# Sparse attention: the 64th largest score of a row found by counting on ScalarE, five units under way, in place of sixteen chunk searches and eight rounds on VectorE

## The chip, the cores and the metric

The kernel runs on one core of a Trainium2 chip. The metric is the device time of one execution in microseconds (us), the median of several runs. PE is TensorE, DVE is VectorE, ACT is ScalarE, POOL is GpSimd, SP is SyncE; PEld is a weight load on PE.

## The reference, cut to what matters

The program is a chain of nine attention, mixture and token layers over `h`, 4 batch rows of 1536 tokens of 64 numbers. The change touches one layer, the sparse attention of layer 2. Its input is `_layernorm(h)`:

```python
value = jnp.einsum('bnd,ed->bne', x, W) + b
norm = jnp.linalg.norm(x, axis=-1, keepdims=True)
normed_x = x / jnp.maximum(norm, EPS)
cos_sim = jnp.einsum('bnd,bmd->bnm', normed_x, normed_x)
topk_vals, topk_inds = jax.lax.top_k(cos_sim, TOP_K)          # TOP_K = 64
attn_sparse = jnp.zeros_like(cos_sim).at[b_idx, n_idx, topk_inds].set(topk_vals)
attn = jax.nn.softmax(attn_sparse, axis=-1)
return jnp.einsum('bnm,bmd->bnd', attn, value)
```

So every token has a row of 1536 similarities; the 64 largest keep their value, the others become 0 (and still count as exp(0) in the softmax).

## The kernel before, in words

A loop takes the four batch rows one after the other (a pass each) through phases; at the end of a phase every engine drains and waits for the others on the semaphore `phase_left`. The order of work inside a phase is written out by hand, engine by engine, and engines meet on counted semaphores (`ph.mark`, `ph.after`). Two phases matter here. `sim2` makes the normed rows `y`, their transpose `qt` (64 partitions by 1536) and `kt`, a copy of it. `attn2` is the sparse attention: 12 units of 128 query tokens.

For unit `u` of `attn2` (functions `attn_pe`, `attn_act`, `attn_vec` with `kind == "attn2"`):

- PE makes three banks of scores (L616) two units ahead; ACT copies the 1536 scores to SBUF (`copy_row`, L760) into one of two row buffers.
- DVE finds the threshold (`maxima`). The row is cut in 16 chunks of 96; each chunk gives its 16 largest by MAX8, MATCH_REPLACE8, MAX8 (L792, L794, L796, `candidates`), 256 candidates together. Eight rounds of MAX8 and MATCH_REPLACE8 over the candidates (L833, L837) give the 64 largest. The chunk searches of unit `u + 1` are issued between the rounds of unit `u`. L842 to L849 test whether the answer could be wrong (`unsure`).
- L850 writes `sparse` = score where it is at least the 64th largest, else 0. PE sums `unsure` over the partitions (L697), DVE loads the sum in a register (L853) and branches: if any row is unsure, the whole 128x1536 tile is searched anew by eight rounds over all 1536 columns (L858, L860). Then `sparse_ready` (L865).
- ACT takes exp of `sparse` with a row sum (L748); PE transposes the result in three groups of four (L645), ACT copies each group (L728), and PE multiplies with the values (L655, the probabilities stationary). DVE scales and adds to `h` (L1102).

## Time and profile before

| | |
|---|---|
| median of 3 runs | 5515.0 us (5504.31 to 5516.92) |
| the profiled execution | 5489.0 us, its span 5487.2 us |
| mean granted TensorE clock | 0.835 |
| busy share of the span | PE 77%, DVE 61%, ACT 35%, POOL 9% |
| one pass of `attn2` in the profile | 701.0 to 984.9 us; four passes |
| DMA | 26.68 MB, mean 5 GB/s |

The profiled execution is 26 us shorter than the median of the three runs. An engine that is busy for a large share of the span bounds the kernel only in the stages in which the others wait for it.

### The profile page before, as it was taken

How to read it: one execution, taken by the hardware profiler on the slowest of the kernel's cores; microseconds unless marked ns; L12 is line 12 of the kernel's file. 1: busy time of each engine (PE TensorE's matmuls, PEld its weight loads, DVE VectorE, ACT ScalarE, POOL GpSimd, SP SyncE). 2: the span in 40 equal slices, each digit the busy share in tenths (PEclk: the TensorE clock that was granted, in tenths of full speed). 3: DMA queues.
4: the chain of work that ended last, by engine and by line, in shares of the span. 5: the costliest groups of instructions: out<-in, count | busy, mean ns of one | idle time of the engine just before them, and what ended most of it. 6: DMA issues, size and time to landing. Idle time of an engine off the chain costs nothing.

```text
span 5487.2 us, 72618 instructions
## 1 busy us (share of the span) xinstructions
PE 4234.8 (77%) x26536; PEld 2887.6 (53%) x26536; DVE 3325.4 (61%) x9095; ACT 1899.6 (35%) x3407; POOL 479.0 (9%) x816
## 2 busy tenths in 40 slices
PE   6885855899887845799888855799888855699987
PEld 4663634565555634555555634555646534555646
DVE  4555689355545679455554779555555769555555
ACT  3341612254341612144332622144432522134432
POOL 0101000101100000011100000011100000021100
PEclk9898955799898965699988966699988976699998
DMA  2000000000000000000000000000000000000000
GB/s 82 5 0 16 4 13 1 1 1 1 1 1 4 1 16 1 1 1 1 1 1 4 1 16 1 1 1 1 1 1 4 1 1 1 1 1 1 1 1 4
DMA packets 28333, 26.68 MB, mean 5 GB/s; under 512 B 10550, under 2 KB 26934, under 8 KB 27450
## 3 DMA queue, kind: packets, MB, share of 16 engines
q1 hardware_dynamic: 27962, 21.98, 1.4%
q8 instruction: 203, 3.33, 0.3%
q14 instruction: 168, 1.38, 0.1%
HBM read 20.40 MB, written 1.57 MB: 4 GB/s over the span
## 4 chain that ended last, share of the span: by engine, by line
PE 52%; DVE 31%; POOL 4%; issue 3%; ACT 2%; DVEq 1%; SPq 0%; POOLq 0%; ACTq 0%
PE ps L605 11%; PE ps L645 7%; DVE qup L794 4%; PE ps L672 4%; PE ps L1622 3%; PE ps L1638 3%; DVE x L792 3%; DVE x L796 3%; DVE ctxt L837 3%; DVE ctxt L833 3%; POOL st L396 2%; PE ps L950 2%; PE ps L608 2%; DVE row_max L1082 2%; PE ps L979 2%
## 5 line engine op out<-in xcount | busy, mean ns | idle before, releaser
L645 PE MATMUL ps<-cst,big 128*128 128x128 f32 x4608 | 660.7, 294 | 313.1 <-ACT big L748 250.3
L645 PEld LDWEIGHTS ps<-cst,big 128*128 128x128 f32 x4608 | 567.7, 153 | 354.8 <-ACT big L748 254.3
L728 ACT COPY big<-ps 128x512 f32<-128x512 f32 x816 | 477.9, 586 | 700.0 <-PE ps L645 696.9
L752 ACT ACTIVATE big<-ps,negmax 128x1024 f32<-128x1024 f32 (+1 forms) x672 | 599.5, 898 | 263.0 <-DVE negmax L867 262.9
L867 DVE TENSOR_REDUCE negmax<-ps 128x1 f32<-128x1536 f32 x336 | 589.9, 1758 | 38.0 <-PE ps L612 18.4
L411 PE MATMUL ps<-cst 128*128 128x512 f32 x608 | 326.9, 697 | 128.0 <-DVEq L187 58.2
L605 PE MATMUL ps<-kup,qup 128*128 128x512 f32 (+3 forms) x768 | 356.3, 561 | 42.1 <-POOLq L187 41.0
L396 POOL TENSOR_TENSOR st<-st,cst 128x6 f32<-128x6 f32 x104 | 156.7, 1507 | 2642.1 <-DVE st L384 2638.0
L424 ACT COPY xt<-ps 64x512 f32<-64x512 f32 x144 | 78.1, 580 | 807.5 <-PE ps L416 807.4
L672 PE MATMUL ps<-big,v 128*32 128x128 f32 (+1 forms) x8064 | 321.9, 277 | 8.1 <-DVE ctxt L1106 6.0
L605 PE MATMUL ps<-klo,qlo 128*128 128x512 f32 (+3 forms) x672 | 313.7, 550 | 3.8 <-DVE big L728 1.5
L411 PEld LDWEIGHTS ps<-cst 128*128 128x128 f32 x608 | 133.4, 227 | 289.6 <-issue 228.7
L760 ACT COPY big<-ps 128x1536 f32<-128x1536 f32 x48 | 69.0, 1438 | 623.3 <-DVE ctxt L865 605.1
L672 PEld LDWEIGHTS ps<-big,v 128*32 128x32 f32 (+1 forms) x8064 | 233.5, 113 | 63.1 <-ACT big L728 53.5
L1082 DVE TENSOR_REDUCE row_max<-ps 128x1 f32<-128x512 f32 (+3 forms) x384 | 213.0, 588 | 76.6 <-PE ps L950 48.9
L655 PEld LDWEIGHTS ps<-v,big 128*128 128x128 f32 x1152 | 254.7, 330 | 0.0
L655 PE MATMUL ps<-v,big 128*128 128x64 f32 x1152 | 252.5, 408 | 0.0
L1986 DVE TENSOR_TENSOR big<-big,ps 85x512 f32<-85x512 f32 x192 | 130.5, 683 | 197.3 <-ACT big L1389 156.8
L728 DVE COPY big<-ps 128x512 f32<-128x512 f32 x336 | 229.0, 682 | 27.1 <-PE ps L645 27.1
L1622 PE MATMUL ps<-cst,big 85*128 85x64 f32 x1536 | 196.1, 285 | 48.7 <-DVE res L1977 48.7
L806 DVE COPY_PREDICATED ps<-cst,ps 128x128 f32<-128x128 int32 x192 | 57.0, 297 | 290.1 <-PE ps L630 290.1
L1622 PEld LDWEIGHTS ps<-cst,big 85*128 85x128 f32 x1536 | 199.4, 204 | 63.1 <-issue 52.9
(321 smaller groups left out, 7413.3 us busy)
## 6 DMA issues: line engine op xcount, KB each, us to landing
rw<-in_w_route SPq DMA_DIRECT2D x128, 64.5 KB, 1.9
cst<-in_consts SPq DMA_DIRECT2D x1, 2671.0 KB, 14.8
cst<-in_consts SPq DMA_DIRECT2D x1, 2670.5 KB, 8.9
big<-in_consts SPq DMA_DIRECT2D x1, 1872.5 KB, 22.1
out_dram<-res SPq DMA_DIRECT2D x4, 384.0 KB, 2.8
experts_in<-in_consts SPq DMA_DIRECT2D x1, 1360.0 KB, 17.6
qup<-in_patches SPq DMA_DIRECT2D x4, 260.0 KB
klo<-in_pe_low SPq DMA_DIRECT2D x2, 384.0 KB, 23.5
```

Of the source, the lines that this page charges most:

```text
L396: nc.gpsimd.tensor_tensor(st[:, 4, t], st[:, 3, t], K("half")[:, t], ALU.pow).then_inc(*ph.mark("rstd_ready"))
L411: nc.tensor.matmul(ps[:, bank, :], ident, K("pos"), start=True, stop=True)
L605: ins = nc.tensor.matmul(bank[:, (a - lo) * P:(b - lo) * P], qq[:, s, qs], kk[:, s, a * P:b * P], start=True, stop=True)
L645: ins = nc.tensor.transpose(turned_bank(kind, u, g)[:, i * P:(i + 1) * P], prob[:, slot_of(kind, u), (4 * g + i) * P:(4 * g + i + 1) * P], ...
L655: ins = nc.tensor.matmul(ps[:, 7, 448:448 + D], pt[:, slot_of(kind, u), g, (i % 4) * P:(i % 4 + 1) * P], v[:, i, :], start=(i == 0), stop= ...
L672: ins = nc.tensor.matmul(ps[w * s:w * s + w, 6, 0:P], v[:, i, at:at + w], pt[:, u % 2, i // 4, (i % 4) * P:(i % 4 + 1) * P], start=(i < n) ...
L728: copy(pt[:, slot_of(kind, u), g, 0:n], turned_bank(kind, u, g)[:, 0:n]).then_inc(*ph.mark(copier(kind, g)))
L752: nc.scalar.activation(prob[:, slot_of(kind, u), cols], src[:, cols], ACT.Exp, bias=bias, accum_out=part_sum[:, u, k:k + 1]).then_inc(*ph. ...
L794: ins = nc.vector.match_replace(work_c, best[:, 0:8], row_c, -4.0)
L867: nc.vector.tensor_reduce(negmax[:, u:u + 1], flat[:, 0:n], AX.X, ALU.max, negate=True)\
L1082: nc.vector.tensor_reduce(row_max[:, lo // 4, unit:unit + 1], ps[:, 5 + n % 2, 0:(hi - lo) * P], AX.X, ALU.max)\
L1622: ins = nc.tensor.matmul(ps[:, 4 + t, e * D:(e + 1) * D], hh[:, n % 2, c, t * P:(t + 1) * P], K("w2_4")[:, (2 * e + c) * D:(2 * e + c + 1) ...
```

## The change

`attn2` gets functions of its own (`sparse_pe`, `sparse_act`, `sparse_vec`), and the 64th largest value is found in another way. For a threshold, ACT computes sign(threshold - score) over the row of 1536 with a running sum (L872 of the new file): the sum tells how many scores lie above it. The first threshold comes from the mean and the deviation of the row (from moments of `y`, not from the scores); DVE then moves it by interpolation between the two ends of a bracket (`move`, some 14 operations on 128 x n numbers, n up to 4), four times at most, until 57 to 64 scores lie above it. After the fifth count one MAX8 over the scores below the threshold gives the values from there to the 64th largest (`select`). If a row of the tile ends outside 57 to 64, the whole tile goes the old way by the eight rounds over 1536 columns. Five units are under way at once: in slot `s` ACT makes the first count of unit `s`, the second of `s - 1`, to the fifth of `s - 4`; then the exp of unit `s - 5`, whose `select` stood in slot `s - 1`, and the copy of row `s + 1`. Six row buffers hold the scores. PE transposes all 12 blocks in one go, ACT copies two of the three banks in one instruction and DVE the third, and the product with the values has the values stationary, as in the other attentions. There are 17 slots for 12 units.

```diff
+PASSES = 5
+ROWS_HELD = PASSES + 1
+START_Z, BRACKET_Z = 1.712, 0.4
+START_COUNT = 40.0
+KEEP = 0.7
...
-        row_copy = (big[:, S:2 * S], big[:, 3 * S:4 * S])
-        sparse = qup[:, 1, :]
+        sparse = work
         qt = qlo[:, 0, :]
-        kt = qlo[:, 1, :]
+        row_copy = (held[:, 0, :], held[:, 1, :], big[:, S:2 * S], big[:, 3 * S:4 * S], qlo[:, 1, :], qup[:, 1, :])
...
+        def counts_in(s):
+
+            return [(s - k + 1, k) for k in (4, 3, 2, 1, 5) if 0 <= s - k + 1 < T]
...
+        def moving(s):
+
+            return max(0, s - PASSES + 2), min(s + 1, T)
...
+        def sparse_pe(ph, pe):
...
+            for t in range(T):
+                ins = nc.tensor.matmul(ps[:, 6 + t // 6, (t % 6) * (D + 1):(t % 6 + 1) * (D + 1)], qt[0:D, t * P:(t + 1) * P],
+                                       moments[0:D, :], start=True, stop=True)
...
+            for s in slots():
+                u, last = s - PASSES, s - PASSES + 1
+                if u >= 0:
+                    pe.wait_ge(*ph.after("probs_ready", u + 1))
...
+                    for i in range(T):
+                        ins = nc.tensor.transpose(ps[:, 3 + i // 4, (i % 4) * P:(i % 4 + 1) * P], prob[:, 0, i * P:(i + 1) * P], ident)
+                    ins.then_inc(*ph.mark("pt_psum"))
+                if s + 2 < T:
+                    scores(s + 2)
+                if u >= 0:
...
+                    for i in range(T):
+                        ins = nc.tensor.matmul(ps[D * (i % 2):D * (i % 2) + D, 6, 0:P], v[:, i, :],
+                                               pt[:, 0, i // 4, (i % 4) * P:(i % 4 + 1) * P],
+                                               start=(i < 2), stop=(i >= T - 2), skip_group_check=True)
+                    ins.then_inc(*ph.mark("strips_ready"))
+                if 0 <= last < T:
+                    pe.wait_ge(*ph.after("unsure_ready", last + 1))
+                    nc.tensor.matmul(ps[:, 7, 0:1], K("mean"), unsure, start=True, stop=True).then_inc(*ph.mark("unsure_summed"))
...
+        def sparse_act(ph, act):
...
+            for s in slots():
+                u = s - PASSES
+                for i, (unit, k) in enumerate(counts_in(s)):
+                    if i == 0:
+                        act.wait_ge(*ph.after("thresholds_ready", s + 1))
+                        act.wait_ge(*ph.after("row_copied", min(s, T - 1) + 1))
...
+                    nc.scalar.activation(counted_out[n % 3], row_copy[unit % ROWS_HELD], ACT.Sign, scale=-1.0, bias=cur[:, 0, unit:unit + 1],
+                                         accum_out=signs[:, unit:unit + 1]).then_inc(*ph.mark("counted"))
+                if u >= 0:
+                    act.wait_ge(*ph.after("sparse_ready", u + 1))
...
+                    nc.scalar.activation(prob[:, 0, :], sparse, ACT.Exp, accum_out=rowsum[:, u:u + 1]).then_inc(*ph.mark("probs_ready"))
+                if s + 1 < T:
+                    copy_row(s + 1)
+                if u >= 0:
+                    act.wait_ge(*ph.after("pt_psum", u + 1))
...
+                    nc.scalar.copy(pt[:, 0, 0:2, :].rearrange("p g n -> p (g n)"), ps[:, 3:5, :].rearrange("p b n -> p (b n)"))\
...
+            def move(s):
...
+                dve.wait_ge(*ph.after("counted", counted_by(s) - (1 if s >= PASSES - 1 else 0)))
...
+            def select(u, s):
...
+                link(nc.vector.scalar_tensor_tensor(work, row, cur[:, 0, u:u + 1], row, ALU.is_lt, ALU.mult))
+                link(nc.vector.max(below[:, 1:9], work))
...
+                link(nc.vector.scalar_tensor_tensor(sparse, row, pick[:, 0:1], row, ALU.is_ge, ALU.mult))
...
-                Phase(led, "attn2").leave(pool)
+                ph = Phase(led, "attn2")
+                pool.wait_ge(*ph.after("var_ready", 1))
+                nc.gpsimd.tensor_tensor(st[:, 4, :], st[:, 3, :], K("half")[:, T:2 * T], ALU.pow).then_inc(*ph.mark("deviation"))
+                ph.leave(pool)
...
                         link(nc.gpsimd.memset(qup[0:D, :, S - 1:S], 0.0))
+                        link(nc.gpsimd.memset(qlo[D:P, 1, :], 0.0))
...
+                for t in range(T):
+                    ins = nc.tensor.matmul(ps[0:D, 0, 0:D], y[:, t, :], y[:, t, :], start=(t == 0), stop=(t == T - 1))
+                ins.then_inc(*ph.mark("square_psum"))
...
-                for j in range(NB):
-                    dve.wait_ge(*ph.after("xt_copied", NB + j + 1))
-                    nc.vector.tensor_copy(kt[0:D, 512 * j:512 * (j + 1)], qt[0:D, 512 * j:512 * (j + 1)])
+                dve.wait_ge(*ph.after("xt_copied", 2 * NB))
+                link(nc.vector.tensor_reduce(moments[0:D, D:D + 1], qt[0:D, :], AX.X, ALU.add))
+                nc.vector.tensor_scalar(moments[0:D, D:D + 1], moments[0:D, D:D + 1], 1.0 / S, None, ALU.mult)
+                dve.wait_ge(*ph.after("square_psum", 1))
+                link(nc.vector.tensor_scalar(moments[0:D, 0:D], ps[0:D, 0, 0:D], 1.0 / S, None, ALU.mult))
```

In the order of the instructions, ACT in the middle of `attn2` before, two units (copy of a row, exp, three group copies):

```order
L760 COPY big<-ps 128x1536 [waits sparse_ready,scores_ready]
L748 ACTIVATE big,rowsum<-qup 128x1536 [waits pt_psum,sparse_ready]
L728 COPY big<-ps 128x512 [waits ctx_ready,pt_psum] x3
L760 COPY big<-ps 128x1536 [waits sparse_ready,scores_ready]
L748 ACTIVATE big,rowsum<-qup 128x1536 [waits pt_psum,sparse_ready]
```

and in the change, one full slot (L872 is a count, L878 the exp, L860 the copy of a row, L885 the copy of two banks):

```order
L872 ACTIVATE y,ctxt<-qlo,ctxt 128x1536 [waits counted,row_copied,thresholds_ready]
L872 ACTIVATE sq,ctxt<-qup,ctxt 128x1536 [waits counted]
L872 ACTIVATE x,ctxt<-held,ctxt 128x1536 [waits counted]
L872 ACTIVATE y,ctxt<-held,ctxt 128x1536 [waits counted]
L872 ACTIVATE sq,ctxt<-big,ctxt 128x1536 [waits counted]
L878 ACTIVATE big,rowsum<-qup 128x1536 [waits pt_psum,sparse_ready]
L860 COPY big<-ps 128x1536 [waits sparse_ready,scores_ready]
L885 COPY big<-ps 128x1024 [waits strips_ready,pt_psum]
```

Five counts have come ahead of the exp; the first waits for the thresholds that DVE moved, and no table load stands between them.

PE for one unit before (L616 scores, L697 the sum of `unsure`, L645 transposes, L655 the product with the values):

```order
L616 MATMUL ps<-qlo 128x512 [waits row_copied]
L616 MATMUL ps<-qlo 128x512 x2
L697 MATMUL ps<-ctxt,cst 128x1 [waits unsure_ready]
L645 MATMUL ps<-cst,big 128x128 [waits pt_by_act,probs_ready]
L645 MATMUL ps<-cst,big 128x128 x3
L645 MATMUL ps<-cst,big 128x128 [waits pt_by_act]
L645 MATMUL ps<-cst,big 128x128 x3
L655 MATMUL ps<-big,v 128x64 [waits ctx_copied,pt_by_act]
```

and in one full slot of the change (L831 transposes, L813 scores, L841 the product with the values, L847 the sum of `unsure`):

```order
L831 MATMUL ps<-cst,big 128x128 [waits pt_by_vec,pt_by_act,probs_ready]
L831 MATMUL ps<-cst,big 128x128 x11
L813 MATMUL ps<-qlo 128x512 [waits row_copied]
L813 MATMUL ps<-qlo 128x512 x2
L841 MATMUL ps<-big,v 64x128 [waits ctx_copied,pt_by_vec,pt_by_act]
L841 MATMUL ps<-big,v 64x128 x11
L847 MATMUL ps<-ctxt,cst 128x1 [waits unsure_ready]
```

The sum of `unsure`, for which DVE waits ahead of its branch, stood ahead of the transposes of its unit before, and now stands behind the scores and the product of the slot.

## Rows read from the trace of the kernel before

**Rows 1.** The page, part 1: busy time, share of the span, instructions.

```profile
PE 4234.8 (77%) x26536; PEld 2887.6 (53%) x26536; DVE 3325.4 (61%) x9095; ACT 1899.6 (35%) x3407; POOL 479.0 (9%) x816
```

**Rows 2.** Windows: busy us of PE, PEld, DVE, ACT, POOL; PEclk; DMA.

```profile
701.00:984.70 283.70, 148.87 (x528) 112.25 (x528) 253.44 (x1164) 56.22 (x72) 0.00 (x0) 0.59 0.01 3
985.00:1985.00 1000.00, 834.52 (x5482) 547.66 (x5482) 543.57 (x1128) 379.50 (x699) 111.36 (x187) 0.89 0.01 4
```

**Rows 3.** Source L850, first pass: durations ns min/median/max, first and last start.

```profile
L850 DVE SCALAR_TENSOR_TENSOR qup<-big,ctxt x12: 1809/1812/1814, 736.1 to 971.2; 128x1536 f32<-128x1536 f32 x12
```

**Rows 4.** Groups by shape, DVE, 705 to 960 us: busy us, mean ns.

```profile
L792 DVE MAX8 x<-big 128x8 f32<-128x96 f32 x192 | 46.3, 304 | 4.6 <-ACT big L760 4.6
...
L837 DVE MATCH_REPLACE8 ctxt<-ctxt 128x256 f32<-128x256 f32 x77 | 31.8, 413 | 0.0
```

**Rows 5.** The same view, ACT, 701 to 985 us, with idle before.

```profile
L760 ACT COPY big<-ps 128x1536 f32<-128x1536 f32 x12 | 17.3, 1438 | 156.1 <-DVE ctxt L865 151.5 <-PE ps L616 4.6
```

**Rows 6.** Timeline, end of a unit: start us, us, engine, line, operation.

```profile
736.00 0.16 DVE L849 TENSOR_TENSOR ctxt<-ctxt 128x1 f32<-128x1 f32 x1
736.08 1.81 DVE L850 SCALAR_TENSOR_TENSOR qup<-big,ctxt 128x1536 f32<-128x1536 f32 x1
...
737.93 0.15 DVE L852 TENSOR_SCALAR ctxt<-ps 1x1 int32<-1x1 f32 x1
739.25 0.15 DVE L865 COPY ctxt<-ctxt 128x1 f32<-128x1 f32 x1 [1.17 <-issue]
...
740.83 1.49 ACT L748 ACTIVATE big<-qup 128x1536 f32<-128x1536 f32 x1
...
742.21 0.19 ACT L748 ACTIVATION_READ_ACCUMULATOR big<-qup 128x1 f32 x1
...
742.46 1.11 PE L645 MATMUL ps<-cst,big 128*128 128x128 f32 x4 [5.65 <-ACT big L748]
```

**Rows 7.** Timeline of PE, a later unit of `attn2`.

```profile
791.68 3.51 PE L655 MATMUL ps<-v,big 128*128 128x64 f32 x16
794.99 4.42 PE L616 MATMUL ps<-qlo 128*128 128x512 f32 x6
```

**Rows 8.** Timeline of PE in `attn0` (values stationary in L672).

```profile
307.55 1.47 PE L645 MATMUL ps<-cst,big 128*128 128x128 f32 x12
308.95 1.53 PE L672 MATMUL ps<-big,v 128*64 128x128 f32 x24
```

**Rows 9.** Window in `attn0`, columns as in rows 2.

```profile
302.00:306.00 4.00, 4.00 (x43) 3.44 (x43) 2.70 (x4) 2.35 (x6) 0.19 (x1) 1.00 0.00 0
```

**Rows 10.** Groups by shape, whole span: the nearest shapes.

```profile
L867 DVE TENSOR_REDUCE negmax<-ps 128x1 f32<-128x1536 f32 x336 | 589.9, 1758 | 38.0 <-PE ps L612 18.4 <-PE ps L608 12.9
L728 DVE COPY big<-ps 128x512 f32<-128x512 f32 x336 | 229.0, 682 | 27.1 <-PE ps L645 27.1
...
L842 DVE MAX8 ctxt<-ctxt 128x8 f32<-128x256 f32 x48 | 20.0, 417 | 0.1
...
L752 ACT ACTIVATE big<-ps,negmax 128x1024 f32<-128x1024 f32 x336 | 374.8, 1115 | 263.0 <-DVE negmax L867 262.9
...
L1054 ACT ACTIVATE big<-ps 128x1024 f32<-128x1024 f32 x120 | 118.9, 1023 | 74.9 <-PE ps L979 57.4 <-PE ps L984 17.4
```

**Rows 11.** Timeline, `sim2` to `attn2`.

```profile
697.46 2.36 PE L416 MATMUL ps<-cst,y 128*64 128x128 f32 x12
...
701.00 5.85 PE L616 MATMUL ps<-qlo 128*128 128x512 f32 x13 [1.18 <-DVEq L187]
```

**Rows 12.** Source L1217, the square root on POOL in `sim2`.

```profile
L1217 POOL TENSOR_TENSOR st<-st,cst x4: 2263/2264/2265, 690.8 to 4452.7; 128x12 f32<-128x12 f32 x4
```

**Rows 13.** Timeline, start of `rel3a`.

```profile
1044.99 2.65 POOL L1229 MEMSET qup<- 64x3072 f32 x1
1045.07 2.60 DVE L1849 TENSOR_SCALAR bias<-bias 80x4 f32<-80x4 f32 x1
```

**Rows 14.** Groups by line, ACT, whole span: table loads.

```profile
L424 ACT ACT_TABLE_LOAD x8 | 10.3, 1283 | 129.2 <-POOLq L161 80.6 <-issue 47.7 <-PEq L2125 0.8
```

More of the change, by code:

```diff
@@ L230, in build @@
         q_more = sb("q_more", [P, 2, S])
+        with nc.sbuf_tensor("held", [P, 2, S], F32) as held:
+            pass
         k_stack = sb("k_stack", [P, 2, S])
@@ L591, in scores @@
                     return
-                if kind != "attn2" and u >= 2:
+                if u >= 2:
                     pe.wait_ge(*ph.after(*copied(kind, u - 2, j)))
-                elif j == 0 and u >= 2:
-                    pe.wait_ge(*ph.after("row_copied", u - 1))
                 bank = ps[:, 3 * (u % 2) + j, :]
@@ L613, in scores @@
                                                start=(part == 0), stop=(part == 1))
-                else:
-                    qq = qt[:, qs]
-                    ins = nc.tensor.matmul(bank[:, 0:(hi - lo) * P], qq, kt[:, lo * P:hi * P], start=True, stop=True)
                 if hi == tiles(kind, q):
@@ L647, in turn @@
                 ins.then_inc(*ph.mark("pt_psum"))
-            def context_2(u, g):
-                pe.wait_ge(*ph.after(*copied(kind, u, g)))
-                if g == 0 and u > 0:
-                    pe.wait_ge(*ph.after("ctx_copied", u))
-                for i in range(4 * g, 4 * g + 4):
-                    ins = nc.tensor.matmul(ps[:, 7, 448:448 + D], pt[:, slot_of(kind, u), g, (i % 4) * P:(i % 4 + 1) * P],
-                                           v[:, i, :], start=(i == 0), stop=(i == T - 1))
-                if g == NB - 1:
-                    ins.then_inc(*ph.mark("ctx_ready"))
             def context(u):
@@ L692, in attn_pe @@
                 ahead = u + 2 < len(units)
-                if kind == "attn2":
-                    for j in range(NB if ahead else 0):
-                        scores(u + 2, j)
-                    pe.wait_ge(*ph.after("unsure_ready", u + 1))
-                    nc.tensor.matmul(ps[:, 7, 0:1], K("mean"), unsure, start=True, stop=True).then_inc(*ph.mark("unsure_summed"))
-                    turn(u, 0)
-                    turn(u, 1)
-                    context_2(u, 0)
-                    turn(u, 2)
-                    context_2(u, 1)
-                    context_2(u, 2)
-                    continue
                 for g in range(NB):
@@ L716, in attn_pe @@
                     side(u + 2)
-            if kind != "attn2":
-                context(len(units) - 1)
-                join(len(units) - 1)
+            context(len(units) - 1)
+            join(len(units) - 1)
         def copy_group(ph, eng, kind, u, g, copy):
@@ L775, in attn_act @@
                         copy_group(ph, act, kind, u, g, nc.scalar.copy)
-                if u + 1 < len(units) and kind != "attn2":
+                if u + 1 < len(units):
                     exps(u + 1)
@@ L867, in maxima @@
+                dve.wait_ge(*ph.after("scores_ready", u + 1))
                 nc.vector.tensor_reduce(negmax[:, u:u + 1], flat[:, 0:n], AX.X, ALU.max, negate=True)\
                     .then_inc(*ph.mark("max_ready"))
-            if kind == "attn2":
-                dve.wait_ge(*ph.after("row_copied", 1))
-                for i in range(CAND_OPS):
-                    candidates(0, i)
-                dve.wait_ge(*ph.own("cand_step"))
-            for u in range(1 if kind == "attn2" else 2):
+            for u in range(2):
@@ L895, in attn_vec @@
             for u in range(len(units)):
-                if kind == "attn2":
-                    if u + 1 < len(units):
-                        maxima(u + 1)
-                    give(u)
-                    continue
                 copy_group(ph, dve, kind, u, 1, nc.vector.tensor_copy)
@@ L908, in attn_vec, with slots, counted_by @@
                     maxima(u + 2)
-            if kind != "attn2":
-                take(len(units) - 1)
-                give(len(units) - 1)
+            take(len(units) - 1)
+            give(len(units) - 1)
+        def slots():
+            return range(T + PASSES)
+        def counts_in(s):
+            return [(s - k + 1, k) for k in (4, 3, 2, 1, 5) if 0 <= s - k + 1 < T]
+        def counted_by(s):
+            return sum(len(counts_in(i)) for i in range(s + 1))
+        def moving(s):
+            return max(0, s - PASSES + 2), min(s + 1, T)
```

293 lines of the change are left out of this document (171 added, 122 removed).

## The prediction

> **What bounds the kernel now.** I read the page's busy shares first [rows 1]: PE is busy 77% of the span, DVE 61%, so over the whole PE seems to lead. The windows by stage say otherwise for the stage that changes [rows 2]: in `attn2` (283.7 us) DVE is busy 253.4 us, 89%, ACT 56.2 us, PE 148.9 us at a granted clock of 0.59 against 0.89 in the 1000 us behind it. The reader is to see one engine full and two waiting. L850 stands once in a unit, and its first and last starts [rows 3] give a unit's period, (971.2 - 736.1) / 11 = 21.4 us. Of ACT's idle time 151.5 us end with DVE's L865 [rows 5], the last step of the search. DVE's time goes into searches of 96 and 256 columns at 304 and 413 ns [rows 4], 48 and 17 of them a unit. So what the stage costs is set by DVE's search, and the change takes that search away.
>
> **What each new piece costs.** A count is an ACTIVATE over 1536 columns in SBUF with a sum, as the exp of L748, 1.49 us, whose sum is read 1.57 us after its start (742.40 - 740.83) [rows 6]. The count's bias is a column; L752 with one takes 1115 ns, L1054 without one 1023 ns [rows 10], so 1.58 us. Its bounds are the row copy, 1.44 us [rows 5], and 1.58 + 0.19 = 1.77 if the read of the sum [rows 6] lay beside nothing; I take 1.57 start to start, since the read overlaps its neighbours in rows 6. Five counts: 7.85 us (7.2 to 8.85). MAX8 over 1536 columns is not in the trace. The step from 96 columns (304 ns, rows 4) to 256 (417 ns) [rows 10] continued gives 1.3 us; the reduction over 1536 takes 1.76 us [rows 10]; I take the latter, since it has the same length. Small DVE operations take 0.16 us [rows 6], about 0.2 where each waits for the last. With this:
>
> - `move`: 9 chained and 6 free small operations, 9 x 0.2 + 6 x 0.1 = 2.4 to 2.6 us.
> - `select`: 0.2 + 1.83 (first pass over the row) + 1.78 (MAX8) + 0.7 + 0.17 (small ones) + 1.81 (the second pass, as L850) + 0.15 + 1.0 for the load and the branch (L852 to L865 is 1.32 from start to start) + 0.15 = 7.7 us [rows 6].
> - PE: twelve transposes at the half clock 3 x 1.11 = 3.3 us [rows 6], at the full clock 1.47 [rows 8]; the product with the values stationary is 24 pieces, 1.53 at full clock [rows 8], 3.1 at half; three scores are six pieces, 4.4 in the middle of a rise [rows 7], 2.7 at full by 13 pieces in 5.85 [rows 11], 5.3 at half.
> - ACT's copy of two banks as L1054, 1.02; DVE's of the third 0.68 [rows 10]; the row copy 1.44 [rows 5].
>
> **The loops of a full slot.** Three things repeat and the longest is the period.
> ACT: 7.85 (counts) + 1.57 (exp) + 3.4 (the transposes, longer than the row copy beside them) + 1.02 = 13.8 us.
> The chain through DVE: exp 1.57, transposes 3.4, third bank 0.68, `select` of the next unit 7.7, a signal 0.1, then its exp: 13.5 us. `move` (2.5) and the output (1 us) are hidden while ACT counts; if DVE were late they would join, and its own work is 7.7 + 2.5 + 0.7 + 1 = 12.
> PE: exp 1.57, transposes 3.4, scores 4.4, product 1.6, the sum of `unsure` 0.6, and DVE's branch 1.3: 12.9 us; wholly at half clock 1.57 + 3.4 + 5.3 + 3.1 + 0.6 + 1.3 = 15.3.
> So a unit takes 13.8 us with a clock that rises in the scores as in rows 7, 15.3 at half while there are scores to make, and 12.0 at full, where ACT's loop is 7.85 + 1.57 + 1.55 + 1.02.
>
> **The stage.** Thresholds: 24 small matmul pieces (0.2 each at half clock) 4.8, DVE 2, the square root on POOL 2.3 [rows 12], DVE 0.5: 9.6 us. Slots 0 to 3: ten counts 15.7, four moves 10, and 6 in which the first scores and row copies are waited for: 41 us. Slot 4 (five counts, a row copy): 50. Slot 5 (7.85 + 1.57 + 3.4 + 4.4 + 1.6 and the output): first unit out at 69.5. Then six units at 13.9, four at 13.5 and the last, with no `select` beside it, at 7.8: 145. Sum 215 us for 284. The same count at half clock throughout gives 226, at full 192.
>
> **Around it.** In `sim2` the three copies to `kt` go, which ran beside the row copies of ACT; twelve matmuls y x y come behind the transposes, which end at 697.46 + 2.36 = 699.8 [rows 11]: 24 pieces at 0.11 to 0.22 us, then a small DVE step, so the phase ends at 702.9 to 705.4 where it ended at 701.0: +2 (to +4.5). In `rel3a` POOL clears 64x1536 more. While it clears 64x3072 in 2.65 us, a DVE operation on 80x4 numbers takes 2.60 us, from 1045.07 to 1047.67, to the end of the clear at 1047.64 [rows 13]; DVE is held there, so half as much again costs 1.3 us, on the path. Nothing is copied by DMA that was not.
>
> **Sum.** A pass: 215 - 284 + 2 + 1.3 = -65.6 us; four passes -262. The profiled execution, 5489.0, becomes 5227; the median of the runs, 5515.0, becomes **5253**. Two executions tell 0.3% (16 us) apart, no less.
>
> **Does the search end in five counts?** The time depends on the data here. I worked the rule of the diff through with the reference's inputs, all 4 x 1536 rows: outside 57 to 64 are 3856 rows after one count, 2204 after two, 309 after three, 17 after four, 0 after five. So no tile of the 48 should take the second search; rounding on the chip may bring one.
>
> **The clock, weighed.** The row: inside a unit before, PE's bursts are cut by waits (5.65 us ahead of L645, rows 6), and the granted clock is 0.59, mostly the 1.2 GHz level; in `attn0`, without a gap, it is 1.00 [rows 9], 2.4 GHz. In the new slot at half clock PE works 12.3 of 15.3 us with gaps of 2 to 3 us, which no stage of rows 2 shows; once at full it works 6.1 of 12.0 us. I take the level between. The Trainium skill (TensorE: Matmul & The Clock Gate, HAM oscillation — how this bites in real kernels) says that a clock falls where bursts are separated by long waits and that each burst then starts cold; by that rule the shorter gaps of the new slot would leave it warm, and the stage would be the 192 us one. The trace neither confirms nor refutes that for gaps so short.
>
> **Rivals.**
> - *Full clock* (17%): 192 us a stage, -91 + 3.4 = -88 a pass, 5515 - 350 = 5165.
> - *Half clock* (17%): 226 us, with the longer `sim2` -54 a pass, 5297. For it: 0.59 now, and every slot still has two waits of PE for DVE.
> - *The three loops do not overlap so well* (9%): they share engines, and a slot becomes 17 us, as if the branch and `move` joined the chain. 12 units cost 3.2 more each, stage 250 to 253, -29 a pass, 5400.
> - *Tables* (3%): sign and exp alternate on ACT. Were they in different tables, two loads of 1283 ns [rows 14] a unit would join ACT's loop: 24 x 1.28 = 31 us a pass, 5377. Against it: no load stands among those instructions in their order. The Trainium skill (ScalarE: Activation LUTs, Table sets: the hidden batching unit) names relu, copy, identity and abs as in every set, and not sign, which speaks for a switch; no run here shows it yet.
> - *The second search runs* (5%), the one on the other side: if thresholds on the chip end outside 57 to 64 for one row of 128, DVE repeats eight rounds over 1536 columns, 16 x 1.76 + 1.8 and 16 drains, some 32 us that nothing covers. The pass breaks even at 65.6 / 32 = 2 tiles of 12. Half the tiles would give 6 x 32 - 65.6 = +126 a pass, 6020 us. Against it the count above; for it, that the row's deviation and ACT's sums must come out on the chip as they do on paper.
>
> My forecast, the mixed clock, has 49%. The range 5165 to 5340 holds it, both clocks and the bounds of a count ((8.85 - 7.85) x 8 slots x 4 = +32 us on 5297); the last three rivals lie above. All cases but the second search are faster by over 0.3%, less 1% for one that comes out between: 94% faster, 1% within 0.3%, 5% slower.
>
> **What the changed profile would show.** The period between two second passes (L960): 13 to 14 us; 15 says PE at half clock, 12 full. L872 at 1.58 us; L954 at 1.76, or 1.3. No L968. PEclk in the stage 0.65 to 0.8. The stage from the first L817 to the last addition to `h` 215 us; 12 exps, no table load. DVE's small operation at the start of `rel3a` 3.9 us. I am wrong if L968 is there, if L872's spacing exceeds 1.8, or if ACT waits most of a slot for `select`.

## The result, and the profile after

The median of the changed kernel is 5233.07 us (5229.57 to 5239.2, 4 runs), that of the kernel before beside it 5511.32 us (5504.31 to 5516.92, 4 runs). The ratio is 0.9497, with a 95% interval of 0.948 to 0.9513: 5% faster. Its profiled execution has a span of 5233.0 us and a mean granted clock of 0.859. The forecast was 5253, with a range of 5165 to 5340. The kernel before was profiled in one of its shorter executions (5489.0 us, 22 under its median), so the medians differ by 278 us and the two profiled spans by 254. What follows is added up in the spans.

Part 1 of the profile's page, for [rows 1]:

```profile
PE 4141.6 (79%) x26824; PEld 2791.7 (53%) x26824; DVE 2849.0 (54%) x6188; ACT 2239.6 (43%) x3791; POOL 494.8 (9%) x824
```

Windows of the first pass's stage and of its middle, columns as in [rows 2]:

```profile
704.40:914.00 209.60, 123.53 (x584) 82.17 (x584) 129.08 (x443) 140.61 (x168) 2.27 (x1) 0.71 0.01 3
752.00:892.00 140.00, 81.38 (x447) 60.81 (x445) 99.16 (x318) 101.66 (x125) 0.00 (x0) 0.67 0.00 1
```

DVE, busy for 253.4 us of the stage before, is busy for 129.1 (4 of them behind the stage's end); ACT went from 56.2 to 140.6. No engine is full any more: in the middle DVE and ACT are both busy for some 100 of 140 us. That is how a loop looks in which two engines hand work to each other. The stage, from the first L817 (704.38) to the end of the last L1193 (909.8), takes 205.4 us where it took 283.9. The source view of L960, the second pass of the select, stands in the place of [rows 3]:

```profile
L960 DVE SCALAR_TENSOR_TENSOR qup<-held,ctxt x4: 1809/1811/1812, 752.4 to 845.4; 128x1536 f32<-128x1536 f32 x4
...
L960 DVE SCALAR_TENSOR_TENSOR qup<-qup,ctxt x2: 1810/1810/1810, 818.7 to 896.9; 128x1536 f32<-128x1536 f32 x2
```

A unit takes (896.9 - 752.4) / 11 = 13.1 us instead of 21.4. The change brings the counting, the five units under way, the twelve transposes in one go and the product with the values stationary together; no run takes them one by one. One full slot in the timeline (start us, us, engine, line, operation):

```profile
782.59 1.47 ACT L878 ACTIVATE big<-qup 128x1536 f32<-128x1536 f32 x1
...
784.05 1.42 ACT L860 COPY big<-ps 128x1536 f32<-128x1536 f32 x1
...
784.20 2.82 PE L831 MATMUL ps<-cst,big 128*128 128x128 f32 x12 [0.77 <-ACT big L878]
...
786.82 4.21 PE L813 MATMUL ps<-qlo 128*128 128x512 f32 x6
787.06 1.01 ACT L885 COPY big<-ps 128x1024 f32<-128x1024 f32 x1 [1.59 <-PE ps L831]
...
787.85 1.81 DVE L953 SCALAR_TENSOR_TENSOR qup<-big,ctxt 128x1536 f32<-128x1536 f32 x1
787.97 1.58 ACT L872 ACTIVATE x<-qup,ctxt 128x1536 bf16<-128x1536 f32 x1
...
789.54 1.57 ACT L872 ACTIVATE y<-held,ctxt 128x1536 bf16<-128x1536 f32 x1
789.69 1.76 DVE L954 MAX8 ctxt<-qup 128x8 f32<-128x1536 f32 x1
...
792.31 1.81 DVE L960 SCALAR_TENSOR_TENSOR qup<-big,ctxt 128x1536 f32<-128x1536 f32 x1
...
795.17 0.15 DVE L975 COPY ctxt<-ctxt 128x1 f32<-128x1 f32 x1 [0.87 <-DVE ctxt L962]
...
795.77 1.47 ACT L878 ACTIVATE big<-qup 128x1536 f32<-128x1536 f32 x1
```

ACT goes round in exp 1.6, wait for the twelve transposes 2.86, two banks 0.9, five counts 7.8: 13.2 us, busy but for the 1.59 us ahead of L885. DVE's L975 ended 0.45 us before the next exp began, so its chain is only that much shorter.

Where the time went is read from the starts of POOL's L408 (L396 before), which ends a normalization in each stage: S reaches from the one in `sim2` to the one in `moe2` and holds the search, M from there to the first in `rel3a`. Every run below is in it, four passes each:

| kernel | S, us | M, us |
|---|---|---|
| before | 304.4, 300.8, 300.8, 300.8 | 61.7, 61.8, 61.7, 61.7 |
| changed | 227.5, 227.5, 254.3, 227.6 | 66.8, 66.7, 66.4, 62.9 |
| changed, again (e0c) | 229.5, 227.5, 254.2, 224.0 | 62.9, 62.9, 66.4, 66.7 |
| e1 half counts | 226.9, 226.8, 226.2, 228.1 | 66.5, 66.5, 66.4, 66.6 |
| e7 no second search | 224.0, 227.4, 226.8, 227.5 | 66.7, 62.9, 66.7, 62.9 |
| e6c four counts | 222.3, 220.3, 220.4, 223.8 | 62.9, 66.4, 66.4, 66.4 |
| e8 one pass more | 247.4, 247.1, 243.5, 243.8 | 62.9, 62.9, 66.4, 62.8 |
| e3 eight idle matmuls | 229.4, 227.6, 254.2, 227.5 | 63.2, 63.5, 63.0, 63.5 |
| e4 clears | 227.6, 224.7, 257.7, 226.0 | 61.6, 65.2, 61.7, 65.4 |
| e5 idle matmuls in the search | 211.9, 208.3, 242.3, 208.6 | 64.0, 66.5, 64.0, 63.9 |
| e10 new order | 205.9, 209.5, 243.1, 205.9 | 62.9, 62.9, 62.9, 62.9 |
| e11c e5 and e10 | 202.7, 202.7, 236.4, 202.8 | 66.4, 66.5, 66.5, 66.5 |
| e9c all that helps | 207.6, 207.7, 210.7, 208.0 | 62.1, 61.7, 62.2, 61.7 |
| e2 always a second search | 605.4, 603.2, 599.8, 603.1 | 66.7, 66.7, 66.7, 66.7 |

S gave 76.9, 73.3, 46.5 and 73.2 us, 270 in all; M took 16 back. Neither the third pass nor M was in the forecast.

S has a part of its own ahead of the search: from L408 to the first matmul of the stage (L616 before, L817 now) were 16.1, 12.8, 12.8 and 12.8 us and are 17.8, 17.8, 14.5 and 17.9. Either kernel has two values there, 3.3 us apart. They go with 24 matmuls of `sim2` that TensorE makes at the one or the other level of its clock; here they are in the second pass, of before and of the changed kernel:

```profile
1948.59 2.89 PE L429 MATMUL ps<-cst,xt 128*128 128x64 f32 x24 [0.67 <-ACT xt L424]
```

```profile
1875.09 5.38 PE L441 MATMUL ps<-cst,xt 128*128 128x64 f32 x24 [0.67 <-ACT xt L436]
```

At like clock `sim2` costs 1.7 us more than before. The values change between executions of one kernel (the first pass of e0c has 18.1, its fourth 14.5), so 3 to 4 us of S in a pass say nothing about the search. The stage itself took 205.4, 205.3, 235.4 and 205.4 us. In the third pass the second search ran, for its unit 10 (timeline of DVE):

```profile
3246.43 1.81 DVE L960 SCALAR_TENSOR_TENSOR qup<-qlo,ctxt 128x1536 f32<-128x1536 f32 x1
...
3248.28 0.15 DVE L962 TENSOR_SCALAR ctxt<-ps 1x1 int32<-1x1 f32 x1
3249.18 1.76 DVE L968 MAX8 ctxt<-qlo 128x8 f32<-128x1536 f32 x1 [0.75 <-DVE ctxt L962]
...
3251.10 1.74 DVE L970 MATCH_REPLACE8 qup<-ctxt,qlo 128x1536 f32<-128x1536 f32 x1
...
3279.04 1.76 DVE L973 SCALAR_TENSOR_TENSOR qup<-qup,qlo 128x1536 f32<-128x1536 f32 x1
...
3290.74 1.81 DVE L960 SCALAR_TENSOR_TENSOR qup<-qup,ctxt 128x1536 f32<-128x1536 f32 x1
```

The next second pass starts 44.3 us later, where the other passes have 12.7 at this place: the search costs 31.6 us and nothing covers it.

### The profile page after: what moved, and what is told of

Read it like the earlier page. It is cut to its first block and busy times, and to the rows that moved or that the text cites. A ratio compares the mean times of both kernels' runs of the same rounds, so it can differ in the third digit from the quotient of the medians.

```text
span 5233.0 us, 70744 instructions
## 1 busy us (share of the span) xinstructions
PE 4141.6 (79%) x26824; PEld 2791.7 (53%) x26824; DVE 2849.0 (54%) x6188; ACT 2239.6 (43%) x3791; POOL 494.8 (9%) x824
## 3 DMA queue, kind: packets, MB, share of 16 engines
HBM read 20.40 MB, written 1.57 MB: 4 GB/s over the span
## 5 line engine op out<-in xcount | busy, mean ns | idle before, releaser
L705 ACT COPY big<-ps 128x512 f32<-128x512 f32 x672 | 394.1, 586 | 494.4 <-PE ps L646 491.4
L646 PE MATMUL ps<-cst,big 128*128 128x128 f32 x4032 | 503.3, 275 | 30.3 <-ACT big L719 29.8
L646 PEld LDWEIGHTS ps<-cst,big 128*128 128x128 f32 x4032 | 457.9, 142 | 48.3 <-ACT big L719 39.7
L436 ACT COPY xt<-ps 64x512 f32<-64x512 f32 x144 | 78.5, 580 | 817.5 <-PE ps L428 817.5
L408 POOL TENSOR_TENSOR st<-st,cst 128x6 f32<-128x6 f32 x104 | 156.9, 1508 | 2306.9 <-DVE st L396 2302.8
L813 PE MATMUL ps<-qlo 128*128 128x512 f32 x288 | 186.4, 799 | 72.3 <-ACT big L860 24.2
L1484 ACT ACTIVATE big<-ps 85x512 f32<-85x512 f32 x192 | 113.8, 594 | 294.3 <-PE ps L1736 294.3
L1145 ACT ACTIVATE big<-ps 128x1024 f32<-128x1024 f32 (+1 forms) x192 | 161.1, 863 | 172.7 <-PE ps L1075 114.6
L592 POOL TENSOR_TENSOR rowsum<-part_sum 128x1 f32<-128x1 f32 x336 | 65.3, 194 | 1687.3 <-ACT big L719 1687.3
```

The lines of the kernel that those rows point to most:

```text
L408: nc.gpsimd.tensor_tensor(st[:, 4, t], st[:, 3, t], K("half")[:, t], ALU.pow).then_inc(*ph.mark("rstd_ready"))
L646: ins = nc.tensor.transpose(turned_bank(kind, u, g)[:, i * P:(i + 1) * P], prob[:, slot_of(kind, u), (4 * g + i) * P:(4 * g + i + 1) * P], ...
L705: copy(pt[:, slot_of(kind, u), g, 0:n], turned_bank(kind, u, g)[:, 0:n]).then_inc(*ph.mark(copier(kind, g)))
L813: ins = nc.tensor.matmul(ps[:, j, :], qt[:, u * P:(u + 1) * P], qt[:, 512 * j:512 * (j + 1)], start=True, stop=True)
L1145: nc.scalar.activation(weight[:, 2 * (m % 4):2 * (m % 4) + 2, off:512], ps[:, 2 * (m % 2):2 * (m % 2) + 2, off:512], ACT.Exp)\
```

## Experiments

### Why did the second search run?

The rule of the diff, worked on the inputs, left no row outside 57 to 64 after five counts. It did not look at one thing: a threshold may be equal to a score. `Sign` of zero adds nothing to the sum, `place` (the count less 56) ends in a half, no element of `iota8` (the whole numbers 8 to 1) is equal to it, and the row passes for one whose search has not ended. **e1** takes a half as well:

```diff
-                link(nc.vector.tensor_scalar(chosen, K("iota8"), place, None, ALU.is_equal))
-                nc.vector.tensor_tensor(near[:, 0, :], chosen, below[:, 0:8], ALU.mult)
-                link(nc.vector.tensor_tensor(near[:, 1, :], chosen, below[:, 1:9], ALU.mult))
+                link(nc.vector.tensor_scalar(chosen, K("iota8"), place, -0.25, ALU.subtract, ALU.add))
+                link(nc.vector.tensor_tensor(chosen, chosen, chosen, ALU.mult))
+                nc.vector.scalar_tensor_tensor(near[:, 0, :], chosen, 0.1, below[:, 0:8], ALU.is_lt, ALU.mult)
+                link(nc.vector.scalar_tensor_tensor(near[:, 1, :], chosen, 0.1, below[:, 1:9], ALU.is_lt, ALU.mult))
```

> The changed kernel ran the second search once, in the third pass (8 MAX8 at L968, 32.6 us from first to last; that pass's stage gained 46.6 us where its neighbours gained 73.3 and 73.2). Theory: a row's last threshold was equal to one of its scores, the sign of zero is zero, the count comes out as a half and no place among the nine values is chosen. Here a half count chooses the place too (one more small VectorE operation per tile, about 0.2 us, nearly all under ScalarE's counts). Theory: no MAX8 of 8 in a row at L968 in any pass, and 25 us less than the changed kernel (5233 to about 5208). Rival, the count lay outside 57 to 64: the second search stays, and the time is 5233 to 5240.

Measured: 5208.57 us, ratio 0.9463 (0.9437 to 0.9489), and no L968 in any pass; S of the third pass is 226.2, like its neighbours. A count outside 57 to 64 would have stayed, so the cause was the equality. The median is 20 us under the changed kernel's in its second measurement (e0c below), a difference that the intervals alone would hardly carry; S of that pass, 28 us shorter, does.

**e7** never takes the search:

```diff
-                nc.vector.tensor_tensor(unsure, pick[:, 1:2], pick[:, 0:1], ALU.is_ge)
+                nc.vector.tensor_scalar(unsure, pick[:, 1:2], 8.0, None, ALU.is_ge)
```

> The test that asks for the second search is made against a constant, so that it is never taken (rows whose search did not end keep whatever the nine values give). Both theories of why it ran: the third pass's stage gains as much as its neighbours, 26.6 us more than the changed kernel, so 5206. If the skipped search was hidden beside other work after all: 5233. It is the base for runs that change the number of counts or VectorE's work.

Measured: 5195.94 us, ratio 0.944 (0.9415 to 0.9466), S of the third pass 226.8. Over four passes S is 2 us under that of e1. The 13 us between the two medians lie elsewhere: M is 7 us shorter and `attn3a`, a stage behind it, 10, while `attn3b` is 5 longer. More on these stages below.

**e2** always takes it (the constant is -8.0):

> The test that asks for the second search is always met: every one of the 48 tiles is searched a second time (the changed kernel did it for one). Theory: a second search costs what the third pass's stage shows, 27 to 28 us, with nothing beside it that could hide it: 47 x 27.6 = 1300 us more than the changed kernel, 6530, slower than the kernel before by 1000; so 10 of 48 tiles would take the whole gain away. Rival: once it is regular, ScalarE's counts of the next tiles lie beside it and the period is VectorE's alone (12.75 + 27.2 us): a little less, 6450 to 6500.

Measured: 6707.71 us, ratio 1.2185 (1.2156 to 1.2213); above the theory, (6707.7 - 5233.1) / 47 = 31.4 us a tile. The second passes of its first two units:

```profile
757.39 1.81 DVE L960 SCALAR_TENSOR_TENSOR qup<-held,ctxt 128x1536 f32<-128x1536 f32 x1
...
802.03 1.81 DVE L960 SCALAR_TENSOR_TENSOR qup<-held,ctxt 128x1536 f32<-128x1536 f32 x1
```

The period is 44.6 us here and 44.3 to 44.7 further on, so the rival with ScalarE's counts beside the search (40) fell too. The 27.6 came from the whole S of the third pass against its neighbours, and that pass was 4.8 us shorter for other reasons: 14.5 us instead of 17.8 ahead of the stage, and 11.4 instead of 12.9 behind the last second pass. The rows of the search itself had said 31.6. The prediction's "some 32 us" was right. About 278 / 31.4 = 9 more tiles of 48 use up the gain.

### What sets the 13.1 us?

**e8** is e7 with L960 made twice, 1.8 us more on DVE's chain and nothing on ACT's loop:

> As the run without any second search, and the second pass of the select (L960, 1.81 us) is made twice. It tells how much room VectorE's chain has beside ScalarE's loop. Theory: 0.4 us of room in the slots that hold five counts, none in the others: +1.5 in seven slots and +1.9 in five, 20 us per pass, 80 in all, from 5196 to 5276. Rival, VectorE binds everywhere: 48 x 1.9 = 91, 5287. Rival, ScalarE binds with 2 us of room, as the page's share of a busy engine would let one think: 5196 to 5230.

Measured: 5279.35 us, ratio 0.959 (0.9575 to 0.9606). **e6c** is e7 without the fifth count, 1.56 us less on ACT's loop and nothing off DVE's chain:

```diff
-            return [(s - k + 1, k) for k in (4, 3, 2, 1, 5) if 0 <= s - k + 1 < T]
+            return [(s - k + 1, k) for k in (4, 3, 2, 1) if 0 <= s - k + 1 < T]
```

> As the run without any second search (5196), and the fifth count of every unit is left out (the threshold then stands one move off, so the select's values are not the ones sought). Theory: ScalarE's loop is the longer one by 0.4 us only, so with one count (1.56 us) less the period goes from 13.2 to VectorE's 12.8, 8 slots x 0.4 x 4 = 13 us: 5183. Rival, ScalarE alone sets the period: 8 x 1.56 x 4 = 50 us: 5146. Rival, VectorE alone: 5196.

Measured: 5196.83 us, ratio 0.9442 (0.942 to 0.9465). The starts of the second pass in the first profiled pass: in full slots of e7 they are 13.18 us apart, each time. With one count less they are 12.78 or 13.08 apart, with one select pass more 14.64 or 14.93, which is 1.85 on each of the two. So DVE's chain takes 12.8 or 13.1, ACT's loop 13.2: ACT leads by 0.4 or 0.1 us, and DVE's chain stands right behind it. S answers: +76 us over four passes for e8 (80 expected), -19 for e6c (13 expected). Of these 19 only 9 lie between the first and the last second pass; 4 lie ahead of the stage, where S has its two values. But the time of e6c does not: of its 19 us, 4 are left in the span (5192.5 against 5196.7), the rest went into M (+3) and `attn3a` (+12). By its total time alone e6c would have spoken for the rival that VectorE sets the period.

### The transposes on the loop

Both loops hold the twelve transposes, 2.82 us at the lower level of the clock. There are two ways to take them off. **e5** keeps TensorE busy:

```diff
+                if u >= 0 and last < T:
+                    keep_clock(3, 2)
                 if 0 <= last < T:
                     pe.wait_ge(*ph.after("unsure_ready", last + 1))
...
+                if u >= 0 and last < T:
+                    keep_clock(3, 2)
                 if u >= 0:
                     pe.wait_ge(*ph.after("strips_copied", u + 1))
...
                         .then_inc(*ph.mark("ctx_ready"))
+                if u >= 0 and last < T:
+                    keep_clock(3, 1)
```

> Five idle multiplications (as L423) per tile stand in TensorE's gaps of the search (two behind the product, two behind the sum of the unsure rows, one behind the joining), into a bank that is free then; nothing waits for them but TensorE's own queue. Theory: half the period's length hangs on TensorE's clock through the 12 transposes alone (2.82 us at the lower level, 1.47 at full), which lie on the loop of ScalarE and on the chain of VectorE alike: granted clock in the stage from 0.71 to 0.9 or more, the period from 13.1 to 11.8, 11 x 1.3 = 14 us per pass, 57 us in all, 5176. Rival A: the idle matmuls delay the sum of the unsure rows and the joining as much as the clock gives: 5233. Rival B: the clock stays at the lower level although the engine is busy: 5233 or more.

Measured: 5175.65 us, ratio 0.941 (0.9393 to 0.9426). Its window of the stage's middle, and a slot of PE:

```profile
752.00:892.00 140.00, 110.70 (x598) 61.14 (x596) 108.14 (x336) 105.60 (x130) 0.00 (x0) 0.97 0.00 1
```

```profile
782.68 1.08 PE L423 MATMUL ps<-cst 128*128 128x512 f32 x2
783.78 1.53 PE L831 MATMUL ps<-cst,big 128*128 128x128 f32 x12
785.15 2.81 PE L813 MATMUL ps<-qlo 128*128 128x512 f32 x6
787.89 1.53 PE L841 MATMUL ps<-big,v 128*64 128x128 f32 x24
```

The granted clock is 0.97 instead of 0.67, the transposes take 1.5 us, and L966 (the second pass here) starts every 11.89 us, 1.3 less. **e10** leaves the clock as it is and changes the order of ACT and DVE:

```diff
+            def two_banks(u):
+
+                act.wait_ge(*ph.after("pt_psum", u + 1))
+                if u >= 1:
+                    act.wait_ge(*ph.after("strips_ready", u))
+                nc.scalar.copy(pt[:, 0, 0:2, :] ...
...
                                          accum_out=signs[:, unit:unit + 1]).then_inc(*ph.mark("counted"))
+                    if i == 0 and u >= 1:
+                        two_banks(u - 1)
...
                 link(nc.vector.scalar_tensor_tensor(work, row, cur[:, 0, u:u + 1], row, ALU.is_lt, ALU.mult))
+                if u >= 1:
+                    turned(u - 1)
...
                     move(s)
-                if u >= 0:
-                    turned(u)
+                if u >= 1:
+                    give(u - 1)
```

> Nothing is added or left out, only the order on two engines is changed: ScalarE takes the two banks of transposed weights (L885) behind the next slot's first count, so that it doesn't stand idle for 1.6 us until the transposes are done; VectorE divides and adds the output (L986, L1193) behind the next move of the thresholds, and takes its bank (L943) behind the first pass of the select. Theory: the transposes leave both loops; ScalarE's becomes the sum of what it does (five counts 7.8, exponentials 1.56, row copy 1.5, two banks 1.0 = 11.9), VectorE's 10.9: the period from 13.1 to 11.8, and 1.9 less in the slots with fewer counts, 17 us per pass, 70 in all, 5163. Rival: the product then comes too late for VectorE's taking of the strips, which holds the next move and so the next counts: 5233 or more.

Measured: 5158.81 us, ratio 0.9382 (0.9362 to 0.9402). ACT in one slot:

```profile
752.25 1.47 ACT L890 ACTIVATE big<-qup 128x1536 f32<-128x1536 f32 x1
...
753.72 1.42 ACT L860 COPY held<-ps 128x1536 f32<-128x1536 f32 x1
755.22 1.58 ACT L882 ACTIVATE sq<-big,ctxt 128x1536 bf16<-128x1536 f32 x1
...
756.79 0.99 ACT L867 COPY big<-ps 128x1024 f32<-128x1024 f32 x1
757.68 1.57 ACT L882 ACTIVATE x<-qlo,ctxt 128x1536 bf16<-128x1536 f32 x1
...
763.93 1.47 ACT L890 ACTIVATE big<-qup 128x1536 f32<-128x1536 f32 x1
```

No idle time stands in brackets: ACT has work from end to end, and its exps are 11.68 us apart (763.93 - 752.25). **e11c** does both:

> The new order and the idle multiplications in the search together. Each alone took about 57 and 74 us off. Theory: they take away the same thing, the 12 transposes at the lower clock on ScalarE's loop; with the new order nothing of TensorE's lies on that loop, so a clock of 0.9 or more in the stage changes the period by nothing (11.7 us) and only the last slots, where VectorE waits for the transposes and the product, get shorter, 2 to 4 us per pass: 5159 to about 5147. Rival, the idle multiplications help by a faster clock everywhere: 5159 - 57 = 5100.

Measured: 5159.35 us, ratio 0.9377 (0.9354 to 0.94), the same as e10. The windows 752 to 836 us, e10's and e11c's:

```profile
752.00:836.00 84.00, 56.15 (x316) 41.33 (x317) 69.55 (x233) 80.77 (x100) 0.00 (x0) 0.72 0.00 1
```

```profile
752.00:836.00 84.00, 71.23 (x379) 40.12 (x380) 68.32 (x224) 81.73 (x100) 0.00 (x0) 0.96 0.00 1
```

A clock of 0.96 instead of 0.72 and ACT as full as before: with the transposes off the loop it moves the unit's period by nothing (11.44 and 11.47 us over eleven units). It shortened S by 20 us over four passes: 11 of them behind the last second pass, 10.1 us instead of 12.9 each time (8 to 16 expected), and most of the rest ahead of the stage, where S has its two values. M took 14 back.

### What moved around the search

**M.** The rows of PE at the start of `moe2`, of before, of the changed kernel's first pass and of its fourth:

```profile
985.05 5.85 PE L411 MATMUL ps<-cst 128*128 128x512 f32 x8 [0.50 <-DVEq L187]
993.25 1.50 PE L416 MATMUL ps<-cst,big 128*64 128x128 f32 x12 [2.35 <-DVE st L406]
```

```profile
909.87 3.70 PE L423 MATMUL ps<-cst 128*128 128x512 f32 x8 [0.50 <-DVEq L190]
918.07 2.77 PE L428 MATMUL ps<-cst,big 128*64 128x128 f32 x12 [4.50 <-DVE st L418]
...
4486.88 5.14 PE L423 MATMUL ps<-cst 128*128 128x512 f32 x8 [0.50 <-DVEq L190]
4495.08 1.50 PE L428 MATMUL ps<-cst,big 128*64 128x128 f32 x12 [3.06 <-DVE st L418]
```

The four idle matmuls (eight pieces) that bridge POOL's root now run at full clock. They end sooner, PE stands for 4.50 us and the next ones run at the lower level: L428 in 2.77 us instead of 1.50, and L1606 behind it in 5.33 instead of 2.93. Where the idle ones happened to run slower (the fourth pass) the clock held. The eleven profiles with four idle matmuls here, of the changed kernel and its variants, agree in all 44 passes: in 29 of them the idle matmuls took 3.70 us, PE stood for 4.5 and L428 took 2.77; in the other 15 PE stood for 3.1 us or less and L428 took 1.50. (Three passes of e5 have L428 at 2.77 and M at only 64.0: L1606 took 2.87 us there.) **e3** makes eight (`keep_clock(0, 8)`):

> The stage behind the search got 3.8, 3.8, 3.5 and -0.1 us longer in the four passes. Theory: its four idle-time multiplications (L423) now run at the full clock, end after 3.7 us instead of 5.85, TensorE stands idle for 4.5 us instead of 2.35, and its clock is at the lower level for the matmuls behind (L428 2.77 us instead of 1.50). With eight of them instead of four the idle time is filled: L428 x12 back to about 1.5 us, 3 x 3.7 = 11 us less than the changed kernel in all (5222). Rival, the stage waits on something else that the search left late (a transfer, VectorE): L428 may be faster but the stage stays as long, 5233.

Measured: 5219.6 us, ratio 0.9483 (0.9456 to 0.951), M 63.0 to 63.5 in all four passes instead of 66.8, 66.7, 66.4 and 62.9: -9.6 us. The total time alone does not tell e3 from the changed kernel (the intervals of the ratio overlap); its rows do:

```profile
914.91 8.73 PE L423 MATMUL ps<-cst 128*128 128x512 f32 x16 [0.50 <-DVEq L190]
923.48 1.47 PE L428 MATMUL ps<-cst,big 128*64 128x128 f32 x12
```

**The clears.** In `rel3a` of the changed kernel (timeline):

```profile
973.63 1.37 POOL L1323 MEMSET qlo<- 64x1536 f32 x1
973.70 1.33 DVE L1949 TENSOR_SCALAR bias<-bias 80x4 f32<-80x4 f32 x1
...
975.06 2.66 POOL L1324 MEMSET qup<- 64x3072 f32 x1
975.09 2.67 DVE L389 TENSOR_SCALAR st<-st 128x6 f32<-128x6 f32 x2
```

Each clear holds one DVE operation to its end, as in [rows 13]. **e4** moves the smaller one, and clears half as much in `sim2`:

```diff
-                clear_upper(ph, pool)
+                nc.gpsimd.memset(qt[D:P, :], 0.0).then_inc(*ph.mark("pool_step"))
+                pool.wait_ge(*ph.own("pool_step"))
...
                 norm_pool(ph, pool, 1)
+                pool.wait_ge(*ph.after("logit_psum", 1))
+                nc.gpsimd.memset(qlo[D:P, 1, :], 0.0)
...
-                        link(nc.gpsimd.memset(qlo[D:P, 1, :], 0.0))
```

> The half of the buffer that the scores' left-hand side has is cleared alone in the stage ahead of the search (one memset of 128... half the bytes, 1.3 us instead of 2.65), and the other half's clearing is moved from the stage behind (1.3 us) into the stage between, where POOL and VectorE wait. Theory: clears held the start of both stages by what they lengthened: -1.3 us ahead of the search and -1.2 us behind it in each pass, 4 x 2.5 = 10 us less than the changed kernel (5223). Rival, both are covered by other work there: stage boundaries as before, 5233. If the moved memset delays the stage between, up to +1.3 x 4 = 5 us more.

Measured: 5228.13 us, ratio 0.9504 (0.9479 to 0.9529), which the total time does not tell from the changed kernel. The rows do. M is 61.6 or 65.2 to 65.4 where it had been 62.9 or 66.4 to 66.8: 1.2 us less at either value. The stretch that ends with the L408 of `sim2` is 5.8 us shorter over four passes, and `attn3a` happened to be 9 us longer. In `sim2` the held operation took 0.45 us instead of 1.73, here of the changed kernel and of e4:

```profile
681.76 1.73 DVE L389 TENSOR_SCALAR st<-st 128x6 f32<-128x6 f32 x2
```

```profile
683.00 0.45 DVE L389 TENSOR_SCALAR st<-st 128x6 f32<-128x6 f32 x2
```

**The same kernel again:**

> The changed kernel as it is, once more, on the chip and in the rounds of the other three, so that they can be set against it directly. The stage behind the search took 59.3 us in three passes and 55.5 in one, without any difference in the work. Theory: TensorE's clock falls there or not by the exact time at which the idle multiplications end, and the other stages with gaps differ in the same way: total 5220 to 5240, with the two values 55.5 and 59.3 in some passes again. If a data-dependent cause is behind it, the same passes have the same values.

Measured: 5228.91 us, ratio 0.9497 (0.9474 to 0.9519). M is 62.9, 62.9, 66.4, 66.7: the same two values in other passes. The stage `attn3a` has two as well, from L408 to L408: 369.4, 369.4, 376.1, 376.1 us in the first profile, 376.2, 375.9, 375.9, 369.3 in this one. The kernel and the data are the same, and the granted clock over `attn3a` is 0.97 where it takes 369.4 and 0.96 where it takes 376. What decides between them is open. In all these runs 369.4 stands only behind an M of 66.7 (63.5 in e3), and `attn3b` is then 158.2 or 158.3 (157.5 in e3), and else mostly 155.8; so what M costs in a pass partly comes back behind it. Against the kernel before, M is 16 us longer and `attn3a` and `attn3b` together 6 shorter. Only the third pass keeps its S (254.3 and 254.2), since its cause is in the data.

### All that helps

**e9c** is e10, e1, e3 and e4 in one:

> The new order on ScalarE and VectorE, the half counts accepted, eight idle multiplications instead of four behind the stage, and the clear moved off the start of the stage behind. Sum of what was measured of each in its place: 5159 for the order, -31 for the second search, -9 for the idle multiplications, -1.2 x 4 = -5 for the clear: 5114. Rival, the pieces meet: the idle multiplications find the clock high already (0 of their 9), 5123; or the half counts' 0.2 us per tile no longer has cover on VectorE, +8, 5122.

Measured: 5126.51 us, ratio 0.9311 (0.9289 to 0.9333). That beats both kernels: 102 us under the changed one measured beside it (e0c), 378 under before. The first rival held (5123). e10 already had M at 62.9 in all passes, so the eight idle matmuls had little to win. Of the second rival there is a trace: the last slots are 0.2 us longer than in e10, 3 us in all. Most of the rest is in `attn3b`, 158.3 to 159.7 us where e10 has 155.8.

## Why the prediction was right

Faster, by 278 us in the medians and 254 in the profiled spans, for 262 forecast in either; 5233 lies 20 us under the 5253. By its own steps:

- *What bounds the kernel*: right. DVE's search set the unit's period; the new search, with all that the change brings along, took 78.5 of 283.9 us away (205.4 left, 215 forecast).
- *Count 1.57, MAX8 1.76, row passes 1.81, two banks 1.02, third bank 0.68*: measured 1.56, 1.76, 1.81, 1.01, 0.69. For MAX8 the reduction of the same length was the right neighbour; the continued line of two short ones (1.3) was not.
- *ACT's loop 13.8 us, DVE's chain 13.5*: measured 13.18 and 12.8 to 13.1. The term that was mis-sized is the twelve transposes, put at 3.3 from three groups of 1.11 and at 3.4 in the loops; in one train of twelve they take 2.82. `select` was put at 7.7 (its terms add up to 7.8) and took 7.6. Which loop leads, and by how little (0.3 forecast, 0.1 to 0.4 measured), was right, and e8 and e6c show it.
- *The mixed clock*: right, 0.71 over the stage (0.65 to 0.8 forecast), 0.67 in its middle. The Trainium skill (TensorE: Matmul & The Clock Gate, HAM oscillation — how this bites in real kernels) describes a clock that falls where bursts stand between long waits, and led me to a rival in which the shorter gaps leave it high; the changed kernel's trace does not bear that rival out, with 0.67 and gaps of up to 3.3 us. In e5, with matmuls in these gaps, the clock was 0.97. The half-clock rival's 5297 does not hold the longer `sim2` that its text names: with -58 + 4.5 + 1.3 a pass it would be 5306, still inside the range.
- *The stage 215*: 205.4. The first output came 65.8 us after the start (69.5 forecast), the other eleven units took 139.6 (145). The first thresholds were ready 7.6 us in, not 9.6: the 24 small matmuls took 2.89, where the prediction had put them at the lower level with 4.8.
- *`sim2` +2*: between the transposes' start and the first matmul of the stage were 3.54 us [rows 11], now there are 5.21, so +1.7 at like clock, in the rows below; the other value of `sim2` made it +5 in two passes, 13 us in all for 8 forecast.

```profile
699.17 2.39 PE L428 MATMUL ps<-cst,y 128*64 128x128 f32 x12
...
701.48 1.61 PE L1594 MATMUL ps<-y 128*64 128x64 f32 x24
702.22 1.75 DVE L1918 TENSOR_REDUCE ctxt<-qlo 64x1 f32<-64x1536 f32 x1 [2.24 <-ACT qlo L436]
...
704.38 2.75 PEld L817 LDWEIGHTS ps<-ctxt,qlo 64*128 64x128 f32 x24 [1.42 <-DVEq L190]
```

  The step behind the y x y matmuls was not small: a sum over all 1536 columns, 1.75 us, is what the stage starts after.
- *`rel3a` +1.3*: 1.2, by the mechanism named; e4 takes it away again.
- *Tables*: no load stands in the stage, and both kernels load 20 times in all. The Trainium skill (ScalarE: Activation LUTs, Table sets: the hidden batching unit) does not name sign among the functions of every set; here it alternates with exp at no cost.
- *The second search does not run*: wrong. It ran for 1 tile of 48 and cost 31.6 us (some 32 forecast). The step that failed is "0 after five. So no tile of the 48 should take the second search": it asked whether a count can be outside the window, and the branch asks whether the place is equal to one of eight whole numbers. A tie of threshold and score gives a half, which e1 shows.
- *Not in the sum at all*: M, +5 us in three passes and +1 in one, of which 1.2 is the clear. The four idle matmuls of `moe2` were long enough (5.6 to 5.9 us) at the clock at which they ran before, and too short at full clock (3.70). What was forecast for the passes, -262, came out as -254 in the spans: -270 in S, +16 in M.

The misses (30 us in the stage of the third pass, 11 for M beside the clear, 5 in `sim2`) and the gain of 9.5 us a stage that was not forecast (38) nearly cancel: -262 - 38 + 46 = -254. That the central number is closer than its parts was luck.

## What to carry to other kernels

When a search moves from one engine to another, write down both engines' loops in full, each with the other's answer in it. A transfer that both loops wait for (here twelve transposes) was worth more, 1.3 to 1.7 us a unit, than one of ScalarE's counts (0.1 to 0.4); moving the wait behind work that is ready (e10, a unit in 11.5 us) gave more than making the awaited work faster (e5, 11.9); the two did not add up. A branch for rare cases needs its exact condition worked out on the data, ties included: one tile of 48 took some 11% of the gain. Idle matmuls are sized for the clock at which they run; a change ahead of them can make them too short.
